# Mixed matrices split by ScalarE and VectorE, the mask multiplied before the mixing, two x loads moved in SyncE's queue

## The reference

```
# layer 0: two of eight experts per batch, and a shared one
x += sum_e dense_w[b,e] * mlp(x, gate[e], up[e], down[e]) + mlp(x, shared)   # gelu(g) * u, width 1024
# layer 1: one mixed matrix per batch
masked_w = weight * mask[None]                 # weight (8, 256, 256), mask (256, 256)
w_bot = einsum('bg,got->bot', cond, masked_w)
x += einsum('bnt,bot->bno', x, w_bot) + bias
# layer 2: a base matrix and eight rank-16 pairs, weighted by cond
x += x @ W_base.T + b_base + 2 * lora(x)
# layer 3: one of eight experts per batch (argmax), silu(up) * gate, width 512
x += mlp3(x, expert[b])
```

## Time and profile before

| what | value |
|---|---|
| median of 3 runs | 1333.11 us (1328.85 to 1336.46) |
| profiled execution, its own time | 1337.89 us |
| its span | 1336.3 us |
| mean granted clock of TensorE | 0.973 |
| busy share: TensorE matmul, weight load | 94%, 85% |
| busy share: VectorE, ScalarE, GpSimd | 53%, 38%, 46% |
| moved by DMA | 119.92 MB, mean 90 GB/s |

### The profile page before, as it was taken

The page is one execution under the profiler, slowest core; times in us unless marked ns, Lnnn a source line. Parts: engine busy times, 40 slices in busy tenths (PEclk is TensorE's granted clock), DMA queues, the critical chain, the costliest instruction groups (busy, mean ns, idle before and its releaser), DMA issues.

```text
span 1336.3 us, 29565 instructions
## 1 busy us (share of the span) xinstructions
PE 1252.7 (94%) x8128; PEld 1135.6 (85%) x8129; DVE 705.2 (53%) x1158; ACT 507.9 (38%) x937; POOL 617.0 (46%) x379
## 2 busy tenths in 40 slices
PE   8989969999999999999999999788888895999998
PEld 7989958888888888888888889788888895887877
DVE  5676535445454454545454544667776774343333
ACT  4456413232223222322322223434444442565554
POOL 1244668026080260807183601865655566888400
PEclk9999979999999999999999999889999998899999
DMA  7267943113031130312131200222222227444211
GB/s 190 76 189 217 298 121 91 31 30 92 16 93 28 31 90 16 92 30 80 42 94 47 90 16 17 79 87 80 87 83 67 67 81 260 144 127 141 78 49 41
DMA packets 132439, 119.92 MB, mean 90 GB/s; under 512 B 64672, under 2 KB 115360, under 8 KB 132384
## 3 DMA queue, kind: packets, MB, share of 16 engines
q1 hardware_dynamic: 115248, 56.82, 15.8%
q0 software_dynamic: 17136, 62.40, 15.1%
HBM read 93.49 MB, written 25.69 MB: 89 GB/s over the span
## 4 chain that ended last, share of the span: by engine, by line
PE 84%; DVE 6%; issue 3%; ACT 2%; DMA 2%; POOL 1%; SPq 1%; DVEq 0%; ACTq 0%; POOLq 0%
PE bank L588 13%; PE bank L589 13%; PE bank L590 13%; PE bank L947 8%; PE bank L640 5%; PE bank L642 5%; PE bank L641 5%; PE bank L625 5%; PE bank L968 4%; PE bank L956 1%; DVE routing L1632 1%; PE bank L684 1%; PE bank L686 1%; PE bank L685 1%; PE bank L809 1%
## 5 line engine op out<-in xcount | busy, mean ns | idle before, releaser
L405 POOL TENSOR_TENSOR Wh<-raw,one 128x1024 fp32r<-128x1024 f32 x79 | 150.3, 1902 | 312.2 <-PE bank L642 287.0
L1480 DVE TENSOR_TENSOR FS<-bank,FS 128x512 f32<-128x512 f32 x200 | 138.0, 690 | 281.5 <-PE bank L590 240.0
L1024 ACT ACTIVATE FS<-bank 128x512 f32<-128x512 f32 x200 | 119.5, 598 | 330.1 <-PE bank L590 329.4
L588 PE MATMUL bank<-Wh,RS 128*128 (+1 forms) x576 | 227.3, 395 | 3.1 <-DVE Wl L1570 2.3
L589 PE MATMUL bank<-Wl,RS 128*128 (+1 forms) x576 | 226.6, 393 | 0.0
L590 PE MATMUL bank<-Wh,RS 128*128 (+1 forms) x576 | 225.2, 391 | 0.0
L407 POOL TENSOR_TENSOR Wl<-raw,Wh 128x1024 fp32r<-128x1024 f32 x79 | 190.8, 2415 | 6.2
L640 PE MATMUL bank<-Wh,RS 128*128 (+1 forms) x576 | 174.3, 303 | 0.0
L642 PE MATMUL bank<-Wh,RS 128*128 (+1 forms) x576 | 162.4, 282 | 0.0
L641 PE MATMUL bank<-Wl,RS 128*128 (+1 forms) x576 | 162.2, 282 | 0.0
L1031 ACT ACTIVATE RS<-bank 128x512 fp32r<-128x512 f32 x144 | 86.1, 598 | 172.4 <-PE bank L625 172.4
(11 more groups left out here) (202 smaller groups left out, 2688.2 us busy)
## 6 DMA issues: line engine op xcount, KB each, us to landing
raw<-in_w POOLq DMA_DIRECT2D x87, 512.0 KB, 4.2
mixes<-acc SPq DMA_DIRECT2D x16, 1024.0 KB, 9.8
raw<-mixes POOLq DMA_DIRECT2D x32, 512.0 KB, 4.2
FS<-in_xT SPq DMA_DIRECT2D x200, 64.0 KB, 2.4
acc<-in_b SPq DMA_DIRECT2D x8, 640.0 KB, 6.5
acc<-x SPq DMA_DIRECT2D x72, 64.0 KB, 2.2
out_rows<-FS SPq DMA_DIRECT2D x72, 64.0 KB, 2.0
acc<-in_x SPq DMA_DIRECT2D x32, 128.0 KB, 3.3
```

The lines of the kernel that those rows point to most:

```text
L405: pool.tensor_tensor(hi, raw[:, k, :], ones_like(PIECE), ALU.mult).then_inc(done, 1)
L588: pe.matmul(ps, ah, bh, start=(i == 0), stop=False)
L1024: act.activation(gl[h], gate_ps[h][:, :], ACT.Gelu_apprx_tanh).then_inc(gelu_done, 1)
L1480: TT(hid[h], up_ps[h][:, :], gl[h], ALU.mult).then_inc(hid_done, 1)
```

## The change

- The host brings the mask into the layout of the stacked w1 pieces (8 x 128 x 1024). GpSimd loads a mask piece into `raw[2]` beside each w1 piece, multiplies in place and signals `masked`; w1 has two buffers left. ScalarE's `stack` waits for `masked` in place of the load. So `mixes` holds masked matrices.
- In the mixed layers `mix_in` with its mask products and low splits is gone; GpSimd keeps the loads (`next_mix`). ScalarE's `mixed_hi` waits for the load and for the layer 1 products that free the buffer. VectorE makes the low parts (`mixed_lo`), right behind `mixed_x`.
- SyncE waits for `tables_ready` earlier and issues the x loads of groups 16 and 17 ahead of the last home loads and spills; the two loads of mask halves are gone.

```diff
@@ block.sync
+            def load_skill(g, p):
+                sp.wait_ge(xl_done, g - 1)
+                load_x(g, p, slot=g - S0)
+
+            sp.wait_ge(tables_ready, 1)
+            for g in range(S0, S0 + 2):
+                load_skill(g, g % 2)
             for pair in range(EARLY - 2, NU):
                 home_x(pair)
             for n in range(WPIECES - 4, WPIECES):
                 spill(n)
-            sp.wait_ge(tables_ready, 1)
-            sp.dma_start(mask1[:, :], mask[1]).then_inc(mask_in, 16)
...
-            with sp.Fori(S0 // 2, S1 // 2) as pair:
+            with sp.Fori(S0 // 2 + 1, S1 // 2) as pair:
                 for k in range(2):
-                    g = 2 * pair + k
-                    sp.wait_ge(xl_done, g - 1)
-                    load_x(g, k, slot=g - S0)
+                    load_skill(2 * pair + k, k)
...
             load_late(1)
-            sp.wait_ge(acc_done, S1)
-            sp.dma_start(maskt[0], mask[0]).then_inc(mask_in, 16)
             load_late(2)
@@ block.gpsimd
-            for m in range(NRAW):
+            for m in range(2):
                 load(m, w1[m])
+                if m == 0:
+                    load(2, mask[0])
...
             for n in range(WPIECES):
-                k = n // 2 % NRAW
+                m, k = n // 2, n // 2 % 2
                 if n % 2 == 0:
-                    pool.wait_ge(raw_in[k], 16 * (n // 6) + 16)
+                    pool.wait_ge(raw_in[k], 16 * (m // 2) + 16)
+                    pool.wait_ge(raw_in[2], 16 * m + 16)
+                    pool.tensor_tensor(raw[:, k, :], raw[:, k, :], raw[:, 2, :], ALU.mult).then_inc(masked, 1)
+                    pool.wait_ge(masked, m + 1)
+                    if m + 1 < WPIECES // 2:
+                        load(2, mask[m + 1])
                 pool.wait_ge(stack_hi, n + 1)
...
-                if n % 2 == 1 and n // 2 + NRAW < WPIECES // 2:
-                    load(k, w1[n // 2 + NRAW])
+                if n % 2 == 1 and m + 2 < WPIECES // 2:
+                    load(k, w1[m + 2])
...
-            def mix_in(n, buffer, after=None):
+            def next_mix(n, u):
                 for i, c in enumerate((1, 0)):
-                    pool.wait_ge(raw_in[c], at_raw[c] + 16 * n + 16)
-                    here = raw[:, c, :].rearrange("p (q b r) -> p q b r", q=8, b=4)
-                    by_batch = maskt[c].rearrange("p (q r) -> p q r", q=8).unsqueeze(2).broadcast_to([P, 8, 4, 32])
-                    pool.tensor_tensor(here, here, by_batch, ALU.mult).then_inc(masked, 1)
-                for i, c in enumerate((1, 0)):
-                    at = MAT + 2 * PIECE * buffer + PIECE * c
-                    pool.wait_ge(mix_hi, 2 * n + i + 1)
-                    pool.tensor_tensor(Wl[:, at:at + PIECE], raw[:, c, :], Wh[:, at:at + PIECE].bitcast(F32),
-                                       ALU.subtract).then_inc(mix_split, 1)
-                    pool.wait_ge(mix_split, 2 * n + i + 1)
-                    if after is not None:
-                        src = mixes[bass.ds(after, 1), :, c * PIECE:(c + 1) * PIECE].rearrange("a p n -> p (a n)")
-                        load(c, src)
+                    pool.wait_ge(mix_split, 2 * n + i - 1)
+                    src = mixes[bass.ds(u, 1), :, c * PIECE:(c + 1) * PIECE].rearrange("a p n -> p (a n)")
+                    load(c, src)
@@ block.scalar
             def stack(n):
-                k, here = n // 2 % NRAW, half_rows(n)
-                if n % 2 == 0:
-                    act.wait_ge(raw_in[k], 16 * (n // 6) + 16)
+                k, here = n // 2 % 2, half_rows(n)
+                act.wait_ge(masked, n // 2 + 1)
...
-            def mixed_hi(n, buffer):
+            def mixed_hi(n, buffer, n_first=True):
                 for i, c in enumerate((1, 0)):
-                    act.wait_ge(masked, 2 * n + i + 1)
+                    act.wait_ge(raw_in[c], AT_RAW_MIX[c] + 16 * n + 16)
+                    if n_first:
+                        act.wait_ge(l1_done, 2 * n - 2)
@@ block.vector
+            def mixed_lo(n, buffer):
+                for i, c in enumerate((1, 0)):
+                    at = MAT + 2 * PIECE * buffer + PIECE * c
+                    dve.wait_ge(mix_hi, 2 * n + i + 1)
+                    TT(Wl[:, at:at + PIECE], raw[:, c, :], Wh[:, at:at + PIECE].bitcast(F32), ALU.subtract)\
+                        .then_inc(mix_split, 1)
...
             x1_lo(0)
+            mixed_lo(0, 0)
...
                 mixed_x(n)
+                mixed_lo(n + 1, 0)
                 keep(n)
...
                 mixed_x(n + 1)
+                mixed_lo(n + 2, 1)
                 keep(n + 1)
```

More of the change, by code:

```diff
@@ L73 @@
 DMA_RING = 6144
+AT_RAW_MIX = [64 + 32 * (E + 1)] * 2
 def build(nc, x, xT, cond, condT, w0, w1, mask, b1, w2, b2, w3, b3, out):
@@ L516, in _ @@
                 pool.memset(t[:, :, S:2 * S].bitcast(F32), 0.0).then_inc(pads_made, 1)
-            pool.wait_ge(mask_in, 32)
-            mix_in(0, 0, after=1)
             pool.wait_ge(raw_in[2], at_raw[2] + 16)
             split(2, L2AT, l2_split, 0)
-            mix_in(1, 1, after=UE)
+            next_mix(1, 1)
             with pool.Fori(1, UL - 1) as k:
-                pool.wait_ge(l1_done, 4 * k - 2)
-                mix_in(2 * k, 0, after=k + 1)
-                pool.wait_ge(l1_done, 4 * k)
-                mix_in(2 * k + 1, 1, after=UE + k)
-            pool.wait_ge(l1_done, 4 * UL - 6)
-            mix_in(2 * UL - 2, 0, after=NU - 1)
-            pool.wait_ge(l1_done, 4 * UL - 4)
-            mix_in(2 * UL - 1, 1)
+                next_mix(2 * k, UE - 1 + k)
+                next_mix(2 * k + 1, k + 1)
+            next_mix(NU - 2, NU - 2)
+            next_mix(NU - 1, NU - 1)
+            for i in range(2):
+                pool.wait_ge(mix_split, 2 * NU)
             at_raw = [at_raw[k] + 16 * NU for k in range(2)]
@@ L1185, in _ @@
             gelu_late(0, 2)
-            mixed_hi(0, 0)
+            act.wait_ge(down_done, 2 * S1)
+            mixed_hi(0, 0, n_first=False)
             hidden_hi_late(0, 1)
@@ L1197, in _ @@
             gelu_late(1, 0)
-            mixed_hi(1, 1)
+            mixed_hi(1, 1, n_first=False)
             def unit(k, xset, last=False):
```

9 lines of the change are left out of this document (4 added, 5 removed).

## The result

| what | before | after |
|---|---|---|
| median of 4 runs each, same chip | 1331.36 us (1328.85 to 1336.46) | 1287.44 us (1287.09 to 1292.68) |
| ratio, 95% interval | | 0.9675 (0.9635 to 0.9714) |
| profiled execution: own time, span | 1337.89, 1336.3 us | 1287.52, 1285.9 us |
| mean granted clock | 0.973 | 0.987 |
| busy share of TensorE, VectorE, ScalarE, GpSimd | 94, 53, 38, 46% | 96, 53, 39, 38% |

The change saves 43.9 us by the medians, 50.4 us between the two profiled executions. The profiled one of before was 6.5 us above its median, so part of the 50.4 belongs to that execution.

What follows compares the result with a forecast made beforehand. TensorE was taken as the bound, its gaps coming from VectorE instructions held while GpSimd works and from a late x load. Terms -23 - 16 - 2 + 8 - 10 = -43 gave 1294.9, carried to the median 1290 us; range 1270 to 1310.

Steps and rivals of the forecast that it cites:

- Steady state: Mixed layers, six units: VectorE no longer held beside GpSimd, TensorE's idle time goes; -23 us, bounds -26.6 and +28.
- The residual of 0.3 us a half: Mixed layers: charge for the part of VectorE's new low splits not covered by TensorE's work, 12 x 0.3 us.
- Start of the layers: 827.0 to 882.6 us: idle time and lower clock go, 1.6 us of the first wait stay; -16 us, bounds -4.4 and -19.4.
- The last two n: End of the mixed layers: -2 us, bounds 0 and -4, GpSimd's splits of layer 3's experts still holding VectorE.
- Mask in the first stage: First stage: eight added GpSimd products make ScalarE's copy late at heads of pairs; +8 us, bounds 0 and +19.
- Handover: Around 170 us: earlier x loads of groups 16 and 17 remove TensorE's wait; -10 us, bounds 0 and -15.2.
- The gap of 3 us: Handover: a sign to look for, a remaining gap of some 3 us that ends with GpSimd's clearing.
- A unit of 32 us for 36: Mixed layers: a sign to look for, each unit taking 32 us in place of 36.
- The clock at 1.00: Mixed layers: a sign to look for, the granted clock at 1.00.
- A: First stage: all eight products go to the path, +19, and the handover gives only 5; 1306 us, chance 0.11.
- B: Mixed layers: ScalarE's crossing copies and `x2_hi` hold TensorE next, half the steady gain remains; 1310 us, chance 0.08.
- C: Mixed layers: VectorE's new splits between z and `x2_lo` are on the path, 2.35 us per n; 1357 us, chance 0.04.

Runs made afterwards that it cites:

- run 6: The change plus a useless GpSimd product reading SBUF behind each load of a mixed matrix, two per n: 1313.78 us, ratio 0.9855.
- run 7: The change plus a GpSimd memset that only writes, behind each load of a mixed matrix, two per n: 1287.90 us, ratio 0.9657.
- run 9: The change plus one useless VectorE subtraction of 1024 columns ahead of the first low split of every n: 1308.58 us, ratio 0.9818.
- run 2: The kernel before with only the x loads of groups 16 and 17 moved up: 1322.87 us, ratio 0.9930.
- run 4: The change without the eight mask products of the first stage, its loads and buffers kept: 1280.94 us, ratio 0.9613.
- run 5: The change with each first-stage mask product between the two low splits of the piece ahead: 1284.55 us; timed again 1286.11 beside the change's 1286.62.
- run 1: The change with the x loads of groups 16 and 17 put back behind home loads, spills and biases: 1298.25 us, ratio 0.9732.
- run 10: The change plus a useless VectorE subtraction ahead of both low splits of every n: 1334.17 us, ratio 1.0020.
- run 3: The kernel before with only the mixed matrices' low splits moved to VectorE, GpSimd keeping both mask products per n: 1295.10 us, ratio 0.9714.

## Why the prediction was right, point by point

The time, 1290 us against 1287.4, and the forecast's mechanism hold. That it came so close is partly luck. The terms sum to -43 us, and the profiles differ by 50.4. The median hides most of that: the forecast took 4.8 us off the profiled time because the profiled execution of before lay that far above its median, but that of the change lies at its own (1287.52 and 1287.44). Against 1294.9 for the profiled execution the miss is 7.4 us, most of it in the first term.

- **Steady state, -23 predicted, -31.8 in the profiles, outside its own bound of -26.6.** The mechanism is shown: `keep` and `join` fell to 0.68 us (after), grow again when GpSimd reads (run 6) and don't when it writes (run 7). The step that failed is the bound. I took TensorE's busy time, 190.3 us for six units, for the least it needs; the same matmuls take 185.1 us. Both stretches behind the 190.3 have clock 1.00, so the clock isn't what it has too much. It is the matmuls beside waits: the last one ahead of a wait is recorded with its full 0.28 to 0.34 us, though the next one otherwise starts 0.12 to 0.18 us later, and the first starts behind a wait follow more slowly. With three waits a unit shows 31.71 us busy, without any 30.90. Run 9 agrees: with two waits of 0.8 us, at clock 1.00, 31.35. Some 4 us of the other difference, 216.9 to 185.1, may be the profiled execution's own (run 2: 212.7).
- **The residual of 0.3 us a half** was not there: no n of the steady part waits. The count behind it was right to a tenth: "covered by some 0.2 us" reads 917.49 against 917.69, and run 9 shows that nearly all of a further split, 1.08 of its 1.2 us, comes to the path.
- **Start of the layers, -16 predicted, -15.3 measured.** 1.6 us of the first wait were to stay; 1.7 did. The clock is 1.00 there for 0.85.
- **The last two n, -2 predicted, -0.2 measured.** TensorE's longest wait there is 7.4 us (7.0 before) for layer 3's first x, which is stored after the last `finish` and loaded again (the L924 row above); the change doesn't touch it. `keep` of the last n fell from 2.82 to 1.19 us beside GpSimd's splits of layer 3's experts, but that saved little: the waits for `x2_lo` are 3.4 us for 3.9. No experiment was made on this stretch.
- **Mask in the first stage, +8 predicted, +10.8 at the last stacked split, +5.5 at the end of the chosen stage (run 4), 6.5 by the medians.** The size holds, the place doesn't. I looked for ScalarE waiting at the heads of pairs; it does wait, 8.4 us in four waits, but run 5 takes these waits away and lies only 0.5 us below the change timed beside it. TensorE's loss is the wait for `mix_out` on VectorE, whose routing instructions are held: the wait of 7.0 us ends with the copy that stands behind the two rows of 2.50 and 2.37 us. With the products this wait is 12.5 us, without them 5.8, and the 6.7 between them is close to the 6.5 of the medians. That the loads and the third buffer cost nothing was right (run 4).
- **Handover, -10 predicted.** Alone it is -12.2 at the end of the chosen stage and -10 by the medians (run 2), and without the product -9.6 (run 4). That the mask half's 4.34 us would leave the queue was wrong (run 1). With the product, part of the first stage's loss is absorbed in it, so the table's -14.9 and +10.8 belong together: -4.1 for the predicted -2. The gap of 3 us that was to end with GpSimd's clearing is not in TensorE's rows: VectorE waits 4.55 us for it, as said ("4.7 us and more"), but TensorE is busy throughout.
- **A unit of 32 us for 36** came out as 30.8. **The clock at 1.00** holds in the start and the steps (0.91 in the last two n).

*The rivals.* A (first stage held, 1306 us) had the right instructions but not the price: 6.5 us and not 19. The rule of the Trainium skill that spoke for it ("SBUF — State Buffer", Who interferes with whom), that a GpSimd instruction which reads SBUF excludes a VectorE one with two SBUF inputs and one that only writes does not, is what runs 6 and 7 show, 1976 against 684 ns for `keep`. B (ScalarE takes the place, 1310) has no row: no steady step waits for ScalarE's copies. C (splits on the path, 1357) did not come, but its deciding point was right. It named a split of twice its row as the point from which the gain is gone; run 10 is that case, and its ratio to before is 1.0020 (1.0007 to 1.0034). The change lives on a margin: 1.2 us more VectorE work per n in this place costs half of the gain (run 9).

## What to carry to other kernels

When VectorE instructions with two SBUF operands show several times their usual duration, look at the same instant for a GpSimd instruction that reads SBUF. Then ask which VectorE instruction stands there: held on the way from TensorE's result to its next operand it cost 26 us with 2.5 us of GpSimd work per n (run 6), beside instructions that read PSUM 4.8 us per n cost nothing in the steady steps (run 3). Moving such work away is a trade, and the place it goes to, the routing of the first stage here, has held instructions too. Don't take the busy time of the bounding engine from a profile with gaps as a floor for the time without them.

## What was not expected of the hardware

- A VectorE COPY with one SBUF operand of 72 numbers is held as well: 2.37 us while GpSimd's product ran (97.55 to 99.88 us), 0.185 us in the kernel before, and so is the CAST of 36 numbers, 2.09 us. The same page and section of the Trainium skill lists copies and casts among what can contend with GpSimd, when their operands meet its conditions. The products and subtractions of VectorE that read one operand in PSUM were never held in these rows: `mixed_x` took 691 to 694 ns in all 16 n of the kernel before.
- Who began first did not decide it in the profile's times: in run 6 `keep` began at 906.35 us, GpSimd at 906.68, and `keep` still took 2.15 us: it ended 0.55 us after GpSimd's product (908.50 and 907.95). The starts of neighbouring VectorE instructions overlap by some 0.1 us in these rows, so this can be an artefact of the records; no run tells.
- The same 2.0 us wait of TensorE in each n (run 10) lets the clock fall in four of twelve steps and not in the others, at a price of 1.5 us each time; with waits of 0.8 us (run 9) it stayed at 1.00 in all twelve steps. What decides it in run 10 stays open.
